# Window attention and convolutions on one core: tokens of two windows interleaved, the 16-bit input copies made per row parity on GpSimd

## The reference

```
xn = group_norm(x)                       # one channel a group
# on each window of 16 x 16 pixels (8 rows of 8 windows):
q, k, v = conv3(xn, qw), conv3(xn, kw), conv3(xn, vw)      # zero padding at the window's edge
q, k, v -> 64 tokens of 128 features (each 2 x 2 block of pixels is a token)
q, k, v = layer_norm(q), layer_norm(k), layer_norm(v)      # gains and biases gq, bq, ...
attn = softmax(q @ k.T * scale + bias)   # 8 heads of 16 features, softmax over 64 keys
xr = xn + pixel_shuffle(attn @ v @ proj_w.T + proj_b)
# on the whole image:
y = xr + conv3(gelu(conv3(xr, c1w)), c2w)
out = x + y
```

## Time and profile before

| | us |
|---|---|
| median of 3 runs | 892.53 (889.89 to 893.34) |
| the profiled execution, its own time | 889.67 |
| its span, first to last instruction | 887.2 |
| TensorE busy | 767.0 |
| VectorE busy | 666.9 |
| ScalarE busy | 664.6 |
| GpSimd busy | 506.1 |

### The profile page before, as it was taken

The page is one execution under the profiler, slowest core; times in us unless marked ns, Lnnn a source line. Parts: engine busy times, 40 slices in busy tenths (PEclk is TensorE's granted clock), DMA queues, the critical chain, the costliest instruction groups (busy, mean ns, idle before and its releaser), DMA issues.

```text
span 887.2 us, 19085 instructions
## 1 busy us (share of the span) xinstructions
PE 767.0 (86%) x5704; PEld 540.5 (61%) x5704; DVE 666.9 (75%) x2142; ACT 664.6 (75%) x1351; POOL 506.1 (57%) x857
## 2 busy tenths in 40 slices
PE   0479999999798999999877999998988899999988
PEld 0256776766356777677534767776734576776753
DVE  6557888878656888887675788887876688887575
ACT  1499999765577999976458999986665899997561
POOL 5558777662426777754153777676242667775510
PEclk9989999999998999999999999999998999999999
DMA  6100032000232130300042013020014112000004
GB/s 240 54 28 28 29 121 87 15 1 1 68 121 61 33 118 5 101 1 1 1 155 72 28 29 121 14 88 1 1 54 132 39 54 75 0 1 1 1 1 142
DMA packets 17658, 47.16 MB, mean 53 GB/s; under 512 B 2081, under 2 KB 2721, under 8 KB 17569
## 3 DMA queue, kind: packets, MB, share of 16 engines
q1 hardware_dynamic: 17568, 46.09, 15.9%
HBM read 37.69 MB, written 8.39 MB: 52 GB/s over the span
## 4 chain that ended last, share of the span: by engine, by line
PE 26%; issue 24%; DVE 21%; ACT 16%; POOL 11%; DVEq 1%; DMA 0%; POOLq 0%; SPq 0%; ACTq 0%
PE y_ps L1004 6%; PE s_ps L1094 5%; POOL ln_rs L723 4%; DVE ln_st L547 4%; ACT ot L832 3%; ACT qk_n L845 3%; PE s_ps L1051 3%; PE o_ps L1072 3%; ACT v_bd L853 3%; PE ox_ps L1020 3%; ACT sc L861 2%; ACT q_m L816 2%; PE y_ps L975 2%; PE pt_ps L1062 2%; DVE h_hi L516 2%
## 5 line engine op out<-in xcount | busy, mean ns | idle before, releaser
L845 ACT ACTIVATE qk_n<-y_ps,ln_nr,ln_rs 128x128 f32<-128x128 f32 x256 | 103.3, 455 | 69.0 <-POOL ln_nr L726 67.8
L1004 PE MATMUL y_ps<-w_hi,x_hi 128*128 128x192 f16 (+1 forms) x512 | 151.1, 295 | 0.0
L1004 PE MATMUL y_ps<-w_lo,x_hi 128*128 128x192 f16 (+1 forms) x512 | 150.4, 294 | 0.0
L1004 PE MATMUL y_ps<-w_hi,x_lo 128*128 128x192 f16 (+1 forms) x512 | 150.3, 294 | 0.0
L701 POOL TENSOR_TENSOR x_lo<-xnf,x_hi 128x448 f16<-128x448 f32 (+1 forms) x128 | 140.3, 1112 | 15.1 <-ACT x_hi L774 15.1
L731 POOL TENSOR_TENSOR sc<-sc,mx 128x512 f32<-128x512 f32 x128 | 133.4, 1042 | 22.7 <-DVE mx L573 22.3
L558 DVE TENSOR_TENSOR sc<-s_ps,biasS 128x512 f32<-128x512 f32 x128 | 86.6, 677 | 59.3 <-PE s_ps L1051 57.3
L1072 PE MATMUL o_ps<-v_bd,pt 128*128 128x66 f32 x1024 | 128.6, 268 | 0.0
L547 DVE BATCH_NORM_STATS2 ln_st<-y_ps 128x6 f32<-128x128 f32 x384 | 88.8, 287 | 52.2 <-PE y_ps L1004 44.9
L1072 PEld LDWEIGHTS o_ps<-v_bd,pt 128*128 128x128 f32 x1024 | 124.5, 192 | 0.2
L723 POOL TENSOR_TENSOR ln_rs<-ln_ve,neg_half 128x3 f32<-128x3 f32 x128 | 112.8, 881 | 10.7
(11 more groups left out here) (160 smaller groups left out, 1619.7 us busy)
## 6 DMA issues: line engine op xcount, KB each, us to landing
xs<-in_x_sh_dram SPq DMA_DIRECT2D x32, 576.0 KB, 3.9
xst<-in_x_al_dram SPq DMA_DIRECT2D x16, 512.0 KB, 7.2
xf<-in_x_al_dram SPq DMA_DIRECT2D x32, 256.0 KB, 4.2
out_dram<-xf SPq DMA_DIRECT2D x32, 256.0 KB, 2.3
wst<-in_wqkv_dram SPq DMA_DIRECT2D x1, 768.0 KB, 3.7
w1s<-in_w_dram SPq DMA_DIRECT2D x1, 256.0 KB, 8.8
w2s<-in_w_dram SPq DMA_DIRECT2D x1, 256.0 KB, 8.8
biasS<-in_bias_t_dram SPq DMA_DIRECT2D x1, 256.0 KB, 9.5
```

The lines of the kernel that those rows point to most:

```text
L845: ins = act.activation(qk_n[j][:, t, :].rearrange("p (h y x) -> p h y x", h=HEADS, y=2), by_head(y_ps[j][:, E * t:E * (t + 1)]), ACT.Identity,
L1004: ins = pe.matmul(y.rearrange("p (t e) -> p t e", t=3)[:, :, cols], xx[r % 2][:, a, P * s:P * (s + 1)], ww[:, a, :].rearrange("p (t e) -> ...
```

## The change

**Layout.** The array that SyncE loads is ordered by pair, by parity z of the pixel row, by row, by column, and last by window of the pair: the tokens of a pair alternate between its two windows. Every offset `a` of the convolution reads one of the two parities (a % 2), at a start that depends on a // 2, so one copy for each parity serves two offsets. `x_hi` and `x_lo` are made by two operations a row of 512 elements each (`high`, `low`, over `rows_of`).

**Engines.** In the steps of an image the high copies of rows 2 to 7 are made by GpSimd (`high`, both where i % 4 is 0), no longer by ScalarE; the low ones follow in the two next steps, one in each. At an image's start the high copies of rows 0 and 1 stay on ScalarE.

**What follows from the order of tokens.** Partitions of the two windows alternate, so v is written by two activations over all 128 partitions, with a scale and a shift that are zero in the partitions of the other window: `ln_vs`, two products of [128,2] on GpSimd for each pair, for which ScalarE waits. Columns of keys alternate by window: `sc` is [head, key, window], the score matmuls write every second column of `s_ps`, q_m and k_m read every second column of `t_ps`, the maximum reads every second element, and the subtraction repeats `mx` in pairs. The DMAs have the same sizes.

```diff
-        x_hi = [sb(f"x_hi{i}", [P, 4, NWIN * TOK], F16) for i in range(2)]
-        x_lo = [sb(f"x_lo{i}", [P, 4, NWIN * TOK], F16) for i in range(2)]
+        x_hi = [sb(f"x_hi{i}", [P, NPAIR, 2, HALF * 2 * TS], F16) for i in range(2)]
+        x_lo = [sb(f"x_lo{i}", [P, NPAIR, 2, HALF * 2 * TS], F16) for i in range(2)]
...
+        def rows_of(t, z):
+
+            return t[:, :, z, 2 * TS * (1 - z):2 * TS * (TS + 1 - z)]
...
-                    v.tensor_reduce(mx[i % 2][:, :, :], sc[i % 4][:, :, :, :], AX.X, ALU.max).then_inc(maxed, 1)
+                    v.tensor_reduce(mx[i % 2][:, :, :], sc[i % 4][:, :, :, :].rearrange("p h k w -> p h w k"), AX.X,
+                                    ALU.max).then_inc(maxed, 1)
...
                 for r in range(2):
-                    for a in range(4):
-                        part(r, a, b * PAIRS, b * NROW, first)
-
-            def part(r, a, p0, r0, first=False):
-
-                pool.wait_ge(xhi_done, (r0 + r) * 4 + a + 1)
+                    for z in range(2):
+                        low(r, z, b * PAIRS, b * NROW, first)
+
+            def high(r, z):
+
+                pool.tensor_copy(rows_of(x_hi[r % 2], z), rows_of(xnf[r % 2], z)).then_inc(xhi_done, 1)
+
+            def low(r, z, p0, r0, first=False):
+
+                pool.wait_ge(xhi_done, (r0 + r) * 2 + z + 1)
                 if r >= 2 or not first:
                     pool.wait_ge(conv_done, p0 + (4 * r - 4))
-                pool.tensor_tensor(at_offset(x_lo[r % 2], a), rows_under(xnf[r % 2], a),
-                                   at_offset(x_hi[r % 2], a), ALU.subtract).then_inc(xlo_done, 1)
+                pool.tensor_tensor(rows_of(x_lo[r % 2], z), rows_of(xnf[r % 2], z), rows_of(x_hi[r % 2], z),
+                                   ALU.subtract).then_inc(xlo_done, 1)
...
+                    pool.tensor_tensor(ln_vs[j][:, 0, :], vec[:, WIN0:WIN1 + 1],
+                                       ln_rs[j][:, 2:3].to_broadcast([P, 2]), ALU.mult)
+                    pool.wait_ge(ln_scales, p0 + (m + 1))
+                    pool.tensor_tensor(ln_vs[j][:, 1, :], vec[:, WIN0:WIN1 + 1],
+                                       ln_nr[j][:, 2:3].to_broadcast([P, 2]), ALU.mult).then_inc(ln_v_scales, 1)
...
-                                       mx[i % 2][:, :, :].unsqueeze(3).to_broadcast([P, HP, 2, TOK]),
+                                       mx[i % 2][:, :, :].unsqueeze(2).to_broadcast([P, HP, TOK, 2]),
                                        ALU.subtract).then_inc(shifted, 1)
                 if 2 <= (i + 8) // 4 < NROW:
-                    for a in ((0,), (1,), (2, 3), ())[i % 4]:
-                        part((i + 8) // 4, a, p0, r0)
+                    if i % 4 == 0:
+                        for z in range(2):
+                            high((i + 8) // 4, z)
+                    for z in ((), (0,), (1,), ())[i % 4]:
+                        low((i + 8) // 4, z, p0, r0)
...
-                if 2 <= (i + 8) // 4 < NROW:
-                    for a in parts_of[i % 4]:
-                        part((i + 8) // 4, a, p0, r0)
...
-                        act.activation(q_m[h % 2][:, :, par, :],
-                                       t_ps[:, 0, :, :].rearrange("p a (w t) -> p (a w) t", w=2), ACT.Identity,
-                                       scale=q_aff[:, par, 0:1], bias=q_aff[:, par, 1:2])
+                        act.activation(q_m[h % 2][:, :, :, par, :], t_ps[:, 0, :, :].rearrange("p a (t w) -> p a w t", w=2),
+                                       ACT.Identity, scale=q_aff[:, par, 0:1], bias=q_aff[:, par, 1:2])
...
+                    act.wait_ge(ln_v_scales, p0 + (m + 1))
                     for w in range(2):
-                        q = slice(64 * w, 64 * w + 64)
                         ins = act.activation(
-                            v_bd[m % 8][q, :, w, 0:2 * HD].rearrange("p h (a y x) -> p h a y x", a=2, y=2),
-                            y_ps[j][q, 2 * E:3 * E].rearrange("p (y h a x) -> p h a y x", y=2, h=HP, a=2),
-                            ACT.Identity,
-                            scale=ln_rs[j][q, 2:3], bias=ln_nr[j][q, 2:3])
+                            v_bd[m % 8][:, :, w, 0:2 * HD].rearrange("p h (a y x) -> p h a y x", a=2, y=2),
+                            y_ps[j][:, 2 * E:3 * E].rearrange("p (y h a x) -> p h a y x", y=2, h=HP, a=2),
+                            ACT.Identity, scale=ln_vs[j][:, 0, w:w + 1], bias=ln_vs[j][:, 1, w:w + 1])
...
-                                            xx[r % 2][:, a, P * s:P * (s + 1)],
+                                            xx[r % 2][:, s, a % 2, 2 * TS * (a // 2):2 * TS * (a // 2 + TS)],
...
-                            out = s_ps[:, half, 0:256].rearrange("p (h w k) -> p h w k", h=2, w=2)
-                            ins = pe.matmul(out[:, :, w, :],
-                                            q_m[h % 2][rows, 2 * (i % 2) + w, :, :].rearrange("p a t -> p (a t)"),
-                                            k_m[h % 2][rows, :, tok], start=True, stop=True)
+                            out = s_ps[:, half, 0:256].rearrange("p (h k w) -> p h k w", h=2, w=2)
+                            ins = pe.matmul(out[:, :, :, w],
+                                            q_m[h % 2][rows, i % 2, w, :, :].rearrange("p a t -> p (a t)"),
+                                            k_m[h % 2][rows, i % 2, w, :, :], start=True, stop=True)
```

More of the change, by code:

```diff
@@ L30 @@
 HROWS = WIN + 2
-HWIN = HROWS * TS
+HALF = TS + 1
+NPAIR = NWIN // 2
 QKV = 3 * E
@@ L41 @@
 GN_BOUND = float(IMG)
-GQ, BQ, GK, BK, GV, BV, PB, C1B, EVEN, ODD, C2B, EVEN2, ODD2 = range(13)
-NVEC = 13
+GQ, BQ, GK, BK, GV, BV, PB, C1B, EVEN, ODD, C2B, EVEN2, ODD2, WIN0, WIN1 = range(15)
+NVEC = 15
 T1R = 5
@@ L150, in conv_attention @@
         ln_nr = [sb(f"ln_nr{i}", [P, 3]) for i in range(2)]
+        ln_vs = [sb(f"ln_vs{i}", [P, 2, 2]) for i in range(2)]
         qk_n = [sb(f"qk_n{i}", [P, 2, P]) for i in range(2)]
         v_bd = [sb(f"v_bd{i}", [P, HP, 2, VW]) for i in range(8)]
-        sc = [sb(f"sc{i}", [P, HP, 2, TOK]) for i in range(4)]
+        sc = [sb(f"sc{i}", [P, HP, TOK, 2]) for i in range(4)]
         mx = [sb(f"mx{i}", [P, HP, 2]) for i in range(2)]
@@ L157, in conv_attention @@
         on = [sb(f"on{i}", [P, 2, HP, HD]) for i in range(2)]
-        q_m = [sb(f"q_m{i}", [P, 4, 2, TOK]) for i in range(2)]
-        k_m = [sb(f"k_m{i}", [P, 2, 2 * P]) for i in range(2)]
+        q_m = [sb(f"q_m{i}", [P, 2, 2, 2, TOK]) for i in range(2)]
+        k_m = [sb(f"k_m{i}", [P, 2, 2, 2, TOK]) for i in range(2)]
         loaded_qkv = sem("loaded_qkv")
@@ L764, in row, with high @@
                 if not first:
-                    act.wait_ge(xlo_done, (r0 + (r - 1)) * 4)
-                act.activation(xnf[r % 2][:, :, :], xs[r % 2][:, :, :], ACT.Identity, scale=xn_aff[:, 0:1],
+                    act.wait_ge(xlo_done, (r0 + (r - 1)) * 2)
+                act.activation(xnf[r % 2][:, :, :, :], xs[r % 2][:, :, :, :], ACT.Identity, scale=xn_aff[:, 0:1],
                                bias=xn_aff[:, 1:2]).then_inc(xn_raw, 1)
-            def part(r, a, p0, r0, first=False):
+            def high(r, z, p0, r0, first=False):
                 act.wait_ge(xn_done, r0 + (r + 1) + 1)
@@ L907, in image @@
                     if followed:
-                        for a in range(4):
-                            part(r, a, (b + 1) * PAIRS, (b + 1) * NROW)
+                        for z in range(2):
+                            high(r, z, (b + 1) * PAIRS, (b + 1) * NROW)
                     for t in (2 * r, 2 * r + 1):
@@ L923, in _ @@
             for r in range(2):
-                for a in range(4):
-                    part(r, a, 0, 0, first=True)
+                for z in range(2):
+                    high(r, z, 0, 0, first=True)
             act.activation(wait_exp[:, :], vec[:, 0:1], ACT.Exp)
@@ L1061, in step @@
                     for g in range(HP):
[L1062 removed]
+                        ins = pe.transpose(pt_ps[:, g, :], sc[m % 4][:, g, :, :].rearrange("p k w -> p (k w)"),
                                            idf[:, :])
@@ L1192, in _lay_out @@
     win[..., 1:-1, 1:-1] = x.reshape(B, C, NROW, WIN, NWIN, WIN).transpose(0, 1, 2, 4, 3, 5)
-    x_sh = np.stack([win[..., c:c + 2 * TS:2] for c in range(4)], axis=1).reshape(B, P, NROW, NWIN * HWIN)
+    x_sh = np.stack([win[..., c:c + 2 * TS:2] for c in range(4)], axis=1)
+    x_sh = x_sh.reshape(B, 4, C, NROW, NPAIR, 2, HALF, 2, TS).transpose(0, 1, 2, 3, 4, 7, 6, 8, 5)
+    x_sh = np.ascontiguousarray(x_sh).reshape(B, P, NROW, NWIN * HROWS * TS)
     e = np.arange(E)
@@ L1219, in _lay_out @@
     bias_t = np.stack([full[:, :, [2 * hp + par for hp in order]] for par in range(2)])
-    bias_t = np.broadcast_to(bias_t.transpose(0, 1, 3, 2)[:, :, :, None, :], (2, TOK, HP, 2, TOK))
+    bias_t = bias_t.transpose(0, 1, 3, 2)[..., None]
+    bias_t = np.broadcast_to(bias_t, (2, TOK, HP, TOK, 2))
```

50 lines of the change are left out of this document (22 added, 28 removed).

## The result

The changed kernel takes **854.66 us** (median of 4 runs, 853.77 to 855.77) against 892.93 for the kernel before beside it (4 runs, 889.89 to 896.02): a ratio of 0.957, 95% interval 0.954 to 0.961. The profiled execution took 854.06 us, its span is 851.9.

What follows compares the result with a forecast made beforehand. No engine was full; a loop of waits between VectorE, GpSimd, ScalarE and TensorE, 18.9 us a row, set the time. Rows -6, later starts -4.5, first start -1.7 made -12.2 us: 880.3 us, range 872 to 898.

Steps and rivals of the forecast that it cites:

- v_bd, the step that failed: ScalarE's v_bd, written by 128 partitions for both windows with as many elements in each partition: costed at nothing.
- The sum for a row: Middle image row: +0.3 (GpSimd, step 1) - 0.6 (ScalarE, step 2) = -0.3 us; 20 rows, -6 us.
- the +0.3: GpSimd: step 0 ends 0.5 us later, of which 0.2 is existing wait; 0.3 us goes into the row's loop.
- -0.6: ScalarE step 2: the x_hi conversion before q_m, 0.59 us, leaves the row's loop.
- Which rows: Gain in the five rows an image of steps 4 to 23; steps 0 to 3 and from 24 on at nothing.
- The starts: Image starts: four x_lo instead of eight on GpSimd free the last two VectorE operations: -1.5 us, three times, -4.5.
- At the first image: First image's start: two of three small VectorE operations before the first statistics freed of x_lo: -1.7 us.
- The costs on GpSimd: f32 to f16 conversion of 512 elements at 0.60 us; two [128,2] products behind ln_nr, +0.3 us for both.
- Rival 1: GpSimd becomes the bound, with casts at contended price (0.85 for 384 elements): +8 us, 900; chance 0.10.
- The layout: Strided maximum, subtraction, q_m, k_m and scores, same element counts: costed at nothing.
- rivals 2 and 3: 2: score matmuls pay for stride, +60, 952, chance 0.12. 3: ScalarE's strided t_ps reads, +4, 896, chance 0.08.
- Rival 4: Loop closes elsewhere: step 2 relief meets TensorE, 1.31 us idle a row; starts give half: -3 to -4, 889; chance 0.15.

Runs made afterwards that it cites:

- v64: Changed kernel with v_bd written by two activations of 64 partitions, first and second half, half its values left out: 870.90 us, ratio 0.976.
- b_v128: Kernel before with only v_bd changed, to two activations over all 128 partitions with masked scales (ln_vs on GpSimd): 877.06 us, ratio 0.984.
- v64_hi_act: Changed kernel with v_bd by two 64-partition activations and the high copies of rows 2 to 7 on ScalarE: 868.26 us, ratio 0.976.
- twice_low: Changed kernel with x_lo of rows 0 and 1 computed twice at each image's start, eight subtractions instead of four: 864.37 us, ratio 0.971.
- hi_act: Changed kernel with the high copies of rows 2 to 7 back on ScalarE, in steps 0 and 1: 854.03 us, ratio 0.957.

## Why the prediction was wrong

**v_bd, the step that failed.** "I cost that at nothing" was for as many instructions of as many elements, and an instruction's duration does bear that out. But I had priced v_bd by its number of elements and not by when the next instruction starts. The two rows for it were at hand: qk_n, two activations of 128 elements on all partitions, 0.81 us with the next at 0.70 us (331.70, 332.40), and v_bd, two of the same size on 64, 0.92 us with the next at 0.95. 0.27 us a pair is 1.08 us a row on ScalarE. One of the four lies in step 2's chain. Measured, it is 16 us of the kernel (v64 against after), 17 (b_v128 against before, 9 to 20 by the interval). This by itself is more than the whole forecast gain.

**The sum for a row.** -0.3 us was right for what it counted: with v_bd undone a row is 18.39 to 18.62 us where it was 18.77 to 18.96 before, 0.34 to 0.38 less, and I had foretold 18.65 for the middle one. Its terms can be read from v64, in the row that ends near 332.01 (compare):

```profile
320.31 0.30 DVE L545 BATCH_NORM_AGGREGATE ln_mv<-ln_st 128x2 f32<-128x6 f32 x3
...
321.00 0.19 POOL L715 TENSOR_TENSOR ln_ve<-ln_mv,eps_y 128x3 f32<-128x3 f32 x1
...
322.69 0.81 ACT L849 ACTIVATE qk_n<-y_ps,ln_nr,ln_rs 128x128 f32<-128x128 f32 x2 [1.80 <-POOL ln_nr L722]
...
326.79 1.54 ACT L836 ACTIVATE ot<-ox_ps 64x256 f32<-64x256 f32 x4
...
330.42 0.69 DVE L551 TENSOR_TENSOR sc<-s_ps,biasS 128x512 f32<-128x512 f32 x1 [1.02 <-PE s_ps L1053]
```

From the end of ln_mv to qk_n it was 1.76 us and is 2.08: the +0.3, since ln_ve starts 0.39 us behind the moments, right behind the conversions, where it was 0.09. From qk_n to the end of ot it was 6.12 and is 5.64: -0.48, not -0.6, for q_m starts 0.66 us behind the start of the exponential and not 0.53, as x_hi did. From there to VectorE's sum it is 2.09 in both. VectorE's own part, from one such sum to ln_mv, went from 8.99 to 8.81, which I had put at nothing; nearly all of it lies around the two memsets of the new layout. So the sum came out right partly because two small errors met. v64_hi_act takes the conversions off GpSimd, and its rows are shorter by 0.11 and 0.14 us, so the +0.3 was a real cost, in part. In the kernel after it is none that shows: as its waits are read above, the loop goes through the normalisation ahead of the conversions.

**Which rows.** The size was off here too. Without the v_bd edit (v64), pairs 12 to 28 give -5.7 us where -0.3 for each of 16 rows makes -4.8: right. But pairs 8 to 12 give -3.7, 0.9 an image; two x_lo of step 2 became one there, which I had put at nothing (argued, not tested). Pairs 4 to 8, steps 0 to 3, give -2.0 where I put nothing. In all, the conversions and starts are 19.9 us of the span in v64, against 12.2 forecast.

**The starts.** Right in size between the images: from the first x_lo to the next image's first product it was 11.4 us (444.54 to 455.94) and is 9.9, the -1.5 forecast; v64 gives -4.3 for all three, against -4.5. It came half by luck. I had both of the last two VectorE operations free of x_lo, 1.5 us, and only the h_lo is: 1.28 + 0.56 us where they took 1.16 + 1.32. The rest is the first h_hi, which now starts 0.15 us ahead of the x_lo (426.74) and takes 0.39 us; before it started 0.07 us behind and took 1.15. TensorE's wait fell by more, 3.1 us, only because its earlier work ended later against the x_lo.

At the first image the step was right and the price too low. From the first x_lo to the first statistics it was 10.1 us, from 28.12, and is 7.7, from 28.05:

```profile
38.25 0.69 DVE L547 BATCH_NORM_STATS2 ln_st<-y_ps 128x6 f32<-128x128 f32 x3
```

```profile
35.75 0.69 DVE L540 BATCH_NORM_STATS2 ln_st<-y_ps 128x6 f32<-128x128 f32 x3
```

That is 2.4 us where I had 1.7: all three small operations of about 1 us are short again, 0.14 to 0.17 us each, and I had counted on two. TensorE's first four pairs show it: 18.1 us before, 16.0 after, 15.9 in v64 and 18.1 again in twice_low. In all, v64's starts give -8.5 us against -6.2: -0.5 up to the first product, -3.8 in pairs 0 to 4, -4.3 between the images. Of the -3.8, 2.3 are the first image's; 1.4 are the fourth image's, where b_v128, which leaves the x_lo alone, has 1.6 too, and their cause stays open.

**The costs on GpSimd.** As forecast. The conversion took 611 ns where I said 0.60, and ln_vs 0.19 with 0.15 between starts:

```profile
L690 POOL CAST x_hi<-xnf 128x512 f16<-128x512 f32 x48 | 28.1, 611 | 0.0
```

Rival 1 (0.85 or more) is out. Which engine makes the conversions makes no difference that hi_act could tell.

**The layout.** As forecast, nothing; rivals 2 and 3 are out. Groups by form of the scores, of q_m and of the maximum:

```profile
L1053 PE MATMUL s_ps<-k_m,q_m 64*128 64x128 f32 x1024 | 92.4, 298 | 1.5 <-issue 1.4
...
L820 ACT ACTIVATE q_m<-t_ps,q_aff 128x256 f32<-128x256 f32 x128 | 65.3, 568 | 4.0 <-PE t_ps L1032 4.0
...
L566 DVE TENSOR_REDUCE mx<-sc 128x8 f32<-128x512 f32 x128 | 87.6, 685 | 4.4
```

The scores' group of eight takes 0.71 us where it took 0.72, the maximum 685 ns as before, q_m 568 ns where it took 560, and 560 in v64, which reads the same columns. The Trainium skill (Advanced Engine Details and Errata, PSUM Cachelines) has any non-contiguous PSUM pattern slow matmuls significantly. These f32 products write every second column and don't bear it out, so the measurement decides.

**Rival 4.** The loop did close elsewhere, with VectorE, but later than its chance assumed: a row had 0.7 us to give before that, and 1.2 with the edges moved, where TensorE is the bound as rival 4 had it.

## What to carry to other kernels

An instruction's cost on an in-order engine is the time from its start to the next one's start; compare that, and not the mean duration, before an edit is costed at nothing. On ScalarE, consecutive activations that alternate between the lower and the upper 64 partitions lose the overlap; one masked activation over all partitions for each costs no more elements and is faster (here at the price of two products of 0.19 us on another engine). When a loop between engines has two chains close to each other, a gain shows up only up to the next one: look for the small instructions on that one (here two memsets of 0.18 us, worth 11 us in all).

## What the runs showed of the hardware

- ScalarE: two activations of 128 elements take 0.92 us, with the next at 0.95, when they lie in different halves of the partitions, and 0.80 to 0.81, with the next at 0.68 to 0.69, when both lie in the same half or in all partitions.
- TensorE's clock at an image's start can fall behind the wait ahead of it. Windows of the wait and of the 3.2 to 3.3 us behind it (the last three columns: granted clock, DMA share, GB/s), of before at the third image, then of after at the third and at the fourth:

```profile
450.00:455.90 5.90, 0.41 (x2) 0.00 (x0) 4.94 (x16) 1.78 (x3) 3.97 (x4) 0.96 0.00 0
455.90:459.20 3.30, 3.26 (x15) 1.94 (x16) 3.23 (x5) 0.00 (x0) 0.00 (x0) 0.56 0.67 215
```

```profile
434.00:436.80 2.80, 0.37 (x2) 0.00 (x0) 2.47 (x7) 0.00 (x0) 0.00 (x0) 1.00 0.00 0
436.80:440.00 3.20, 3.18 (x21) 1.88 (x21) 3.13 (x5) 0.00 (x0) 0.00 (x0) 1.00 0.67 216
```

```profile
638.40:640.90 2.50, 0.08 (x1) 0.00 (x0) 2.31 (x5) 0.00 (x0) 0.00 (x0) 0.96 0.00 0
640.90:644.10 3.20, 3.16 (x13) 1.94 (x14) 3.13 (x5) 0.00 (x0) 0.00 (x0) 0.50 0.65 214
```

After 5.5 us of waiting TensorE ran mostly at half of its 2.4 GHz, 1.2, for the next 3 us and got through 15 products in it. After 2.5 us it once ran at full clock and got through 21, and once, in the same execution, at half with 13. Over the ten traces, each of the 15 waits of 3.9 to 5.5 us at the later images' starts had a stretch at half clock behind it (granted 0.50 to 0.71 over 3.2 us), and 4 of the 15 waits of 2.5 to 2.7 us had. So a wait can slow the work behind it, more often a long one, and its length alone doesn't say whether.
